# Four small tiles of a graph kernel moved from SBUF into idle PSUM banks, and the x rows taken six tiles later in each stage

## The reference, cut to what matters

```
w     = 1 / max(edge_attr_2[:, 0], 1e-6)
slope = edge_attr_2[:, 1] * w
diff  = (x[dst] - x[src]) * w[:, None]
d1    = segment_sum(diff, dst) - segment_sum(diff, src)
S     = segment_sum(slope, dst)
u     = x - dt * (x * d1 + g * S);  x = layernorm(x + u)
x     = layernorm(x + segment_sum(edge_attr_16, dst) / count(dst))
```

## Time and profile before

| what | value |
|---|---|
| time, median of three runs | 4502.62 us (4499.23 to 4514.22) |
| the profiled execution | 4499.55 us, span 4497.7 us |
| granted TensorE clock, mean | 0.995 |
| PE busy | 4398.7 us, 98% |
| POOL busy (gathers) | 3423.2 us, 76% |
| DVE busy | 3895.9 us, 87% |
| ACT busy | 1458.3 us, 32% |

### The profile page before, as it was taken

How to read it: one execution, slowest core, us unless ns; L and a number is a source line. 1 busy time by engine, 2 the same in 40 slices (tenths; PEclk the granted TensorE clock), 3 DMA queues, 4 the chain that set the end, 5 groups by cost and what they waited for, 6 DMA issues and landing times. The chain is left out here.

```text
span 4497.7 us, 73977 instructions
## 1 busy us (share of the span) xinstructions
PE 4398.7 (98%) x31379; PEld 1230.3 (27%) x12630; DVE 3895.9 (87%) x8605; ACT 1458.3 (32%) x1018; POOL 3423.2 (76%) x3133
## 2 busy tenths in 40 slices
PE   4999999999999999999999999999999999999997
PEld 1222222222222222222222222222222222222222
DVE  6888888888888888888888888888888888888887
ACT  4333333333333333333333333333333333333321
POOL 7777777777777777777777777777777777777770
PEclk9999999999999999999999999999999999999998
DMA  3111111111111111111111111111111111111110
GB/s 92 37 35 41 36 35 37 35 42 35 37 35 35 42 35 37 35 41 36 35 37 35 42 35 36 36 35 42 35 37 35 38 39 35 37 35 40 38 25 8
DMA packets 210291, 167.80 MB, mean 37 GB/s; under 512 B 124650, under 2 KB 193774, under 8 KB 210024
## 3 DMA queue, kind: packets, MB, share of 16 engines
q1 hardware_dynamic: 109798, 139.79, 10.1%
q0 software_dynamic: 100000, 25.80, 6.7%
q10 hardware_dynamic: 476, 2.01, 0.1%
HBM read 164.55 MB, written 2.81 MB: 37 GB/s over the span
## 5 line engine op out<-in xcount | busy, mean ns | idle before, releaser
L430 POOL DMA_INDIRECT x_src<-in_x_dram,src_i x3125 | 3418.3, 1094 | 961.8 <-issue 900.5
L656 PE MATMUL ps_src<-hi_hot,spread_lo 128*128 128x392 bf16 (+1 forms) x18750 | 4117.3, 328 | 0.0
L1004 DVE TENSOR_SCALAR hi_hot<-col_h,hi_f,scale 128x1564 bf16<-128x1564 f16 x3125 | 2173.7, 715 | 18.1 <-PE ps_src L656 14.8
L651 PE MATMUL ps_src<-hi_hot,spread_lo 128*128 128x392 bf16 x6250 | 2050.4, 328 | 19.2 <-DVE hi_hot L1004 9.8
L651 PEld LDWEIGHTS ps_src<-hi_hot,spread_lo 128*128 128x128 f16 x6250 | 614.9, 98 | 1022.0 <-issue 611.9
L604 PEld LDWEIGHTS ps_w<-dst_hots,parts 128*102 128x102 bf16 x3125 | 393.7, 127 | 977.1 <-issue 939.5
L593 PEld LDWEIGHTS ps_x<-xwin,nodes_mem 112*128 112x128 bf16 x3125 | 300.8, 97 | 1196.4 <-issue 1187.1
L983 DVE TENSOR_TENSOR spread_lo<-spread_lo,halves 128x640 f16<-128x640 f16 x1250 | 609.3, 496 | 0.0
L593 PE MATMUL ps_x<-xwin,nodes_mem 112*128 112x48 bf16 x3125 | 580.2, 188 | 13.9 <-ACT nodes_mem L533 13.9
L604 PE MATMUL ps_w<-dst_hots,parts 128*102 128x112 bf16 x3125 | 499.9, 213 | 4.0 <-DVE parts L912 4.0
L523 ACT CAST parts<-left 128x400 bf16<-128x400 f32 x125 | 71.5, 572 | 1206.8 <-DVE left L945 1206.8
(11 more groups left out here) (119 smaller groups left out, 1128.5 us busy)
## 6 DMA issues: line engine op xcount, KB each, us to landing
rel_all<-rel_d SPq DMA_DIRECT2D x125, 800.0 KB
x_src<-in_x_dram,src_i POOLq DMA_INDIRECT x3125
a<-in_edge_attr_dram SPq DMA_DIRECT2D x125, 200.0 KB, 2.4
a<-in_edge_attr_dram SPq DMA_DIRECT2D x125, 25.0 KB
src_i<-in_src_dram SPq DMA_DIRECT2D x125, 12.5 KB
dst_i<-in_dst_dram SPq DMA_DIRECT2D x125, 12.5 KB, 1.7
xwin<-xparts_d SPq DMA_DIRECT2D x125, 10.5 KB
dst_sum<-in_dst_dram SPq DMA_DIRECT2D x1, 1400.0 KB
```

The lines of the kernel that those rows point to most:

```text
L430: nc.gpsimd.indirect_dma_start(x_src[:, b, j * F:(j + 1) * F], None, x[:, :], bass.IndirectOffsetOnAxis(ap=src_i[:, b, j:j + 1], axis=0)). ...
L651: return nc.tensor.matmul(out_bank, weights, moving, start=False, stop=stop)
L656: return nc.tensor.add_instruction(mybir.InstMatmult(name=nc.get_next_instruction_name(), engine=pe.engine, start_tensor_calc=False, stop_ ...
L1004: v.tensor_scalar(hi_hot[:, slot(j), 0:HOT], col_h[:, 0:HOT], hi_f[:, b, j:j + 1], scale[:, b, j:j + 1], ALU.is_equal, ALU.mult).then_inc( ...
```

## The change

`x_dst` and `pay` become one PSUM tile in the bank of `ps_w`, from column 64; `scaled` moves into bank 1 of `ps_x` and `left` into bank 2. So VectorE writes four tiles into PSUM, and VectorE and ScalarE read them there. What shares `left` with the attributes gets an SBUF tile of its own, `attr_rest`, and the slopes one called `slope`, from which VectorE copies them into `pay` ahead of `diff`. The rows of x go into tiles 6 to 18. New waits keep the banks apart.

```
+        PAY0 = P // 2
+        pay = ps_w[:, PAY0:PAY0 + J * (F + 1)].rearrange("p (j v) -> p j v", v=F + 1)
+        x_dst = pay[:, :, 0:F]
+        scaled = ps_x[:, 1, 0:J * F].rearrange("p (j f) -> p j f", f=F)
+        left = ps_x[:, 2, 0:J * (F + 1)].rearrange("p (j v) -> p j v", v=F + 1)
+        attr_rest = sb("attr_rest", [P, J, F], f32)
+        slope = sb("slope", [P, J], f32)
-        SUM_AT, ROWS_AT = 11, 0
+        SUM_AT, ROWS_AT = 11, 6
+        BANK_AT = ROWS_AT + PER // 2
 # TensorE, in stage
+                    if j == BANK_AT and begin:
+                        pe.wait_ge(parts_ready, c + 2)
 # TensorE, ahead of the first stage
             pe.wait_ge(x_dst_added, 1)
+            pe.wait_ge(parts_ready, 1)
             x_of_dst(1)
 # VectorE: x_of_dst
+                    if not (isinstance(n, int) and n == 0):
+                        dve.wait_ge(win_added, n)
 # VectorE: diff
+                    dve.wait_ge(slope_ready, n + 1)
+                    step(v.tensor_copy(pay[:, :, F], slope[:, :]))
                     dve.wait_ge(gathered[b], (k + 1) * 16 * J)
 # VectorE: scale
-                    dve.wait_ge(pay_ready, n + 1)
+                    dve.wait_ge(part0_ready, n + 1)
 # VectorE: parts
                     step(v.tensor_tensor(halves[:, :, 1, :], scaled, halves[:, :, 0, :], ALU.subtract))
                     done["half1"] = count[0]
+                    settle_here()
                     dve.wait_ge(left_ready, n + 1)
                     dve.wait_ge(part1_ready, n + 1)
-                    v.tensor_tensor(parts[:, :, 2, 0:F + 1], left[:, :, 0:F + 1], parts[:, :, 1, 0:F + 1], ALU.subtract).then_inc(parts_ready, 1)
+                    v.tensor_tensor(parts[:, :, 2, 0:F + 1], left, parts[:, :, 1, 0:F + 1], ALU.subtract).then_inc(parts_ready, 1)
```

More of the change, by code:

```diff
@@ L94, in gnn_kernel @@
         w = sb("w", [P, J], f32)
-        x_dst = sb("x_dst", [P, J, F], f32)
         x_dst_more = sb("x_dst_more", [P, J, F], f32)
-        left = sb("left", [P, J, ONE], f32)
-        pay = sb("pay", [P, J, F + 1], f32)
+        attr_rest = sb("attr_rest", [P, J, F], f32)
+        slope = sb("slope", [P, J], f32)
         parts = sb("parts", [P, J, SPL, V], bf16)
@@ L106, in gnn_kernel @@
         unscale = sb("unscale", [P, J], f32)
-        scaled = sb("scaled", [P, J, F], f32)
         hi_hot = sb("hi_hot", [P, RING, HCOL], bf16)
@@ L139, in gnn_kernel @@
         PER = 10
+        PAY0 = P // 2
+        assert PAY0 + J * (F + 1) <= 512
+        pay = ps_w[:, PAY0:PAY0 + J * (F + 1)].rearrange("p (j v) -> p j v", v=F + 1)
+        x_dst = pay[:, :, 0:F]
+        scaled = ps_x[:, 1, 0:J * F].rearrange("p (j f) -> p j f", f=F)
+        left = ps_x[:, 2, 0:J * (F + 1)].rearrange("p (j v) -> p j v", v=F + 1)
         TPB = 512 * 4 // (P * 2)
@@ L306, in gnn_kernel @@
         FIRST_HALF = ["dst_rel", "slope"]
-        A_STEPS, B_STEPS, W_STEPS = 2, 19, 1
+        A_STEPS, B_STEPS, W_STEPS = 2, 20, 1
         NSTEP = A_STEPS + B_STEPS + W_STEPS
@@ L510, in finish @@
                 act.wait_ge(left_ready, n + 1)
-                nc.scalar.copy(parts[:, :, 1, 0:F + 1], left[:, :, 0:F + 1]).then_inc(part1_ready, 1)
+                nc.scalar.copy(parts[:, :, 1, 0:F + 1], left[:, :, :]).then_inc(part1_ready, 1)
                 if not (isinstance(n, int) and n == 0):
@@ L522, in attr_parts @@
                 act.wait_ge(attr_left_ready, m + 1)
-                nc.scalar.copy(parts[:, :, 1, F + 1:2 * F + 1], left[:, :, F + 1:2 * F + 1]).then_inc(attr1_ready, 1)
+                nc.scalar.copy(parts[:, :, 1, F + 1:2 * F + 1], attr_rest[:, :, :]).then_inc(attr1_ready, 1)
             def node_hot(m, b):
@@ L867, in finish @@
                     dve.wait_ge(attr1_ready, n + 1)
-                    v.tensor_tensor(parts[:, :, 2, F + 1:2 * F + 1], left[:, :, F + 1:2 * F + 1], parts[:, :, 1, F + 1:2 * F + 1], ALU.subtract)
+                    v.tensor_tensor(parts[:, :, 2, F + 1:2 * F + 1], attr_rest[:, :, :], parts[:, :, 1, F + 1:2 * F + 1], ALU.subtract)
                 if piece == "lo":
@@ L886, in finish @@
                     settle_here()
-                    v.tensor_tensor(pay[:, :, 0:F], x_dst[:, :, :], bc(w[:, :], 2, F), ALU.mult).then_inc(pay_ready, 1)
+                    v.tensor_tensor(pay[:, :, 0:F], x_dst, bc(w[:, :], 2, F), ALU.mult).then_inc(pay_ready, 1)
                 if piece == "scale":
-                    dve.wait_ge(pay_ready, n + 1)
+                    dve.wait_ge(part0_ready, n + 1)
                     step(v.tensor_reduce(top[:, :], pay[:, :, 0:F], AX, ALU.max, apply_absolute_value=True))
@@ L900, in finish @@
                     settle_here("unscale")
-                    v.tensor_tensor(scaled[:, :, :], pay[:, :, 0:F], bc(unscale[:, :], 2, F), ALU.mult).then_inc(scaled_ready, 1)
+                    v.tensor_tensor(scaled, pay[:, :, 0:F], bc(unscale[:, :], 2, F), ALU.mult).then_inc(scaled_ready, 1)
                 if piece == "left":
                     dve.wait_ge(part0_ready, n + 1)
-                    v.tensor_tensor(left[:, :, 0:F + 1], pay[:, :, :], parts[:, :, 0, 0:F + 1], ALU.subtract).then_inc(left_ready, 1)
+                    v.tensor_tensor(left, pay, parts[:, :, 0, 0:F + 1], ALU.subtract).then_inc(left_ready, 1)
                 if piece == "parts":
@@ L907, in finish @@
                     dve.wait_ge(half0_ready, n + 1)
-                    step(v.tensor_tensor(halves[:, :, 1, :], scaled[:, :, :], halves[:, :, 0, :], ALU.subtract))
+                    step(v.tensor_tensor(halves[:, :, 1, :], scaled, halves[:, :, 0, :], ALU.subtract))
                     done["half1"] = count[0]
+                    settle_here()
                     dve.wait_ge(left_ready, n + 1)
                     dve.wait_ge(part1_ready, n + 1)
-                    v.tensor_tensor(parts[:, :, 2, 0:F + 1], left[:, :, 0:F + 1], parts[:, :, 1, 0:F + 1], ALU.subtract).then_inc(parts_ready, 1)
+                    v.tensor_tensor(parts[:, :, 2, 0:F + 1], left, parts[:, :, 1, 0:F + 1], ALU.subtract).then_inc(parts_ready, 1)
                 if piece == "rel2":
@@ L944, in attr_left @@
                 dve.wait_ge(attr0_ready, m + 1)
-                v.tensor_tensor(left[:, :, F + 1:2 * F + 1], a16[:, b, :].rearrange("p (j f) -> p j f", f=F),
+                v.tensor_tensor(attr_rest[:, :, :], a16[:, b, :].rearrange("p (j f) -> p j f", f=F),
                                 parts[:, :, 0, F + 1:2 * F + 1], ALU.subtract).then_inc(attr_left_ready, 1)
@@ L997, in begin @@
                     dve.wait_ge(dve_step, base_step + count[0])
-                    v.tensor_tensor(pay[:, :, F], a2[:, b, 1:2 * J:2], w[:, :], ALU.mult).then_inc(slope_ready, 1)
+                    v.tensor_tensor(slope[:, :], a2[:, b, 1:2 * J:2], w[:, :], ALU.mult).then_inc(slope_ready, 1)
             def one_hot(c, b, j):
```

## The result

The changed kernel takes **4495.31 us** (median of 8 runs, 4494.98 to 4495.67), the kernel before, on the same chip, 4507.75 us (8 runs, 4499.23 to 4515.19). The ratio is 0.9974 with an interval of 0.9965 to 0.9984: 12 us faster, where I forecast 3 us slower. The two spreads matter as much as the medians: 0.7 us after, 16 us before. The profiled executions, 4499.55 before and 4495.52 after, are only 4.0 us apart; the one of before was among its fastest.

A forecast was written before the change was run, and what follows sets the result against it. TensorE and POOL's gathers were taken as two full engines. TensorE +1, chain +1.7 and start +0.5 gave +3.2 us on 4499.55, 4502.8; with the median 3.1 us above that execution, 4506 us, range 4494 to 4532.

The forecast's parts named there:

- the third rival: POOL's gathers get quicker with six fewer VectorE operations on two SBUF tiles per chunk; 4491 to 4499 us, 12%.
- POOL was not full: On POOL, the forecast counted busy time plus 0.30 us per gather as 1994 us, 99.7% of the stretch: a full engine.
- TensorE: On TensorE, 15 instead of 3 halves hold a sum and a row, with no visible surcharge; +1 us.
- VectorE's chain: From `diff` to `parts` on VectorE, the settle adds 0.11 us and PSUM operands 0.04; +0.15 us, bounds -0.1 and +1.0.
- What a longer chain costs: Chain growth d costs 11 late stages d, 41 middle ones d - 0.21, 71 ordinary ones d - 0.90; +1.7 us.
- The second rival, slow PSUM: Bank conflicts or a fixed cost per PSUM operation stretch VectorE's chain by 0.6 to 1.0 us; 4524 to 4552 us, 14%.
- The late stage becomes the rule: A slightly moved chain makes every stage lose the late one's 0.43 us; +53 us, 4556 us, 6%.
- Start: In chunk 0 `scale` starts up to 2.9 us later, hidden by TensorE's 8.00 us stop; +0.5 us comes through.

The follow-up runs named there:

- h1: Kernel before, TensorE held until chunk 1's gathers are in, chunk 2's gathers not gated, eight surplus rounds of rows of x; 4510.97 us, ratio 1.0023.
- e1: Changed kernel with x of dst, payload, scaled payload and rest back in SBUF, all else kept; 4605.74 us, ratio 1.0242.
- e4: Changed kernel with only `scaled` and `left` back in SBUF, payload and x of dst staying in PSUM; 4615.26 us, ratio 1.0254.
- h2: Changed kernel with all four tiles back in SBUF and without the added settle ahead of `parts`; 4507.03 us, ratio 1.0013.
- e5: Kernel before, TensorE held once ahead of stage 0 until POOL has issued five gathers of chunk 2, which is not gated; 4942.85 us, ratio 0.9999.
- g1: Kernel before, TensorE held until chunk 1's gathers are in, chunk 2's not gated, eight surplus rounds of rows of x; 4949.54 and 9450.36 us.

## Why the prediction was wrong, point by point

**The step that failed** is the third rival's dismissal: "The one-hot explains the delay alone, and it stays." I read one gather beside L901. That row was right, L901 holds only 3 of 122; but I took it for all operations with two SBUF sources, and `left` holds 87 of 119, the second half 29 of 32. One look at the gather beside L904, of 2.1 us, would have contradicted it. The mechanism that I gave 12%, at 4491 to 4499 us, is the one that happened, though of the six operations that it counts two do nearly all the holding that I counted. I also gave the rule of the Trainium skill's page "SBUF — State Buffer" (section "SBUF: two separate sides") no more weight than that one row let it have.

**POOL was not full.** I worked out 1564.54 + 1430 x 0.30 = 1994 us and called it a full engine, from which followed "112 of 123 stages recover by themselves". The sum is right and its reading wrong: POOL's busy time includes being held, and is the length of the stage because POOL and VectorE are in step. h1 shows the same 1564.5 us in that stretch, 17 us ahead and with nobody waiting. After has 1521.91 us, and 0.76 us of each chunk at its gates besides.

**TensorE: right.** Forecast +1 us for 12 more mixed halves, measured 34.987 against 34.980, +0.9. A half with two sums and a row takes 2015.47 - 2014.69 = 0.78 us against the 0.79 of the earlier trace rows.

**VectorE's chain: nearly.** Forecast +0.15 us, measured +0.21; the settle was costed right (0.60 us from L921 to L926). Writing to PSUM is free: the group means after, against the earlier trace rows (568 for L887 is 569 for L900, 644 is 654):

```profile
L917 DVE TENSOR_TENSOR ps_x<-ps_w,parts 128x425 f32<-128x425 f32 x125 | 74.8, 599 | 0.0
...
L900 DVE TENSOR_TENSOR ps_w<-ps_w,w 128x400 f32<-128x400 f32 x125 | 71.2, 569 | 0.0
L897 DVE TENSOR_TENSOR ps_w<-ps_w,x_src 128x400 f32<-128x400 f32 x125 | 70.8, 567 | 14.3 <-DMA x_src<-in_x_dram,src_i 14.3
```

**What a longer chain costs: wrong sign.** "The 11 late stages pay d" held the distribution of places fixed. With POOL gone ahead, `diff` no longer waits for it, and the chain, 0.21 us longer, ends 1.92 us early. The term was forecast at +1.7 us and is -5.0 us in the profiled pair; with TensorE's +0.9 and the start's +0.15 that makes the 4.0 us between them. It is larger against the median, since the profiled execution of before had few late stages: its runs spread over 16 us, those of after over 0.7. That all of the other 8 us of the medians is late stages is argued from these spreads, not traced. The room that I had started from was also too large: its median over the stages before is 0.65 us, where I had put 71 of 123 stages at 0.90.

**The second rival, slow PSUM: refuted** (+10 ns at most on an operation). The fixed costs of the Trainium skill's page "VectorE: DVE Perf Modes" (section on the TRN2 errata), by my estimate some 65 ns more from PSUM, are not seen here.

**"The late stage becomes the rule": real, but not in this kernel.** I had argued that a tenth of a microsecond on the chain could turn it into the rule. In e1 and e4 it did, at 0.95 us a stage, twice my 0.43 and +106 and +116 us for my +53; h2 shows that it takes the settle. The change brings this cost and, by its placement, the cure. Both were in my list; I weighed them as alternatives where they stand one behind the other.

**Start: right.** `scale` starts at 50.71 instead of 47.66, 3.05 us later for my 2.9, and TensorE's long stop hides it:

```profile
78.58 0.51 PE L657 MATMUL ps_src<-hi_hot,spread_lo 128*128 128x392 bf16 x1 [9.53 <-DVE hi_hot L1018]
```

The first two stages and what precedes them come to 144.83 us after and 144.69 before, +0.15 unrounded for my +0.5. No gain came from the start.

## What to carry to other kernels

Where one engine issues gathers in software and another writes tiles beside it, an engine sum of 99.7% may be two engines in step: look where a chunk ends within the stage, and if it is the same few places each time, some meeting holds it. Before one row decides against a mechanism, read the same meeting for each operation of the kind. And judge two small effects on one such knife edge together: a settle of 0.1 us cost 2.3% with the tiles in SBUF, and with them in PSUM, the settle there too, no stage from the third on was late by it.

## What the runs showed of the hardware that I had not expected

- A gather that a one-hot has stopped can be held further by a VectorE operation with two SBUF sources, 0.5 to 1.0 us each time, and never (0 of 123 for `left`) when one source is in PSUM; `left` holds with its output in either place. Why `scaled` holds so seldom, `left` so often and `spread` never (0 of 196) stays open.
- A gather that is held by a one-hot ends 0.82 us behind it where it began 0.2 to 0.5 us after it, and 0.2 to 0.3 us behind it where it began earlier.
- POOL, which no semaphore held in h1, kept VectorE's step of 34.98 us at -17.1 us from the fourth stage to the last. In the kernel before the places are about +0.37 us, but there VectorE waits for the gathers in every stage.
- VectorE's writes to PSUM cost as much as those to SBUF to 10 ns. ScalarE's cast of 425 elements is quicker from PSUM: 545 ns for 579.
- On one of the chips the kernel before took 4944 and 4922 us instead of 4500 to 4508; e5, traced there, has TensorE standing for "issue", and POOL's pace holds nobody up. Why the settle slows e1 by as much as it does, and why g1 once took twice its time, stays open.
